# A fused two-layer residual kernel: rows of the gated blocks 8 KB apart in DRAM instead of 2 KB

## The chip, the cores and the metric

The kernel runs on one core of a Trainium2 chip. Its engines are TensorE (PE in the profile, with its weight loads as PEld), VectorE (DVE), ScalarE (ACT), GpSimd (POOL) and SyncE (SP, which here only issues transfers). Transfers between DRAM and the on-chip memories run on 16 DMA engines that all queues share. The metric is the time of one execution on the device in microseconds (us). The kernel before took 1368.03 us, the median of three runs (1366.42 to 1370.3).

## What is computed

The input x has 8 sequences of 1024 positions with 512 channels, all in 32-bit floats. Two layers are added to it in turn. Cut to what matters:

```python
# layer 0: an adapter chosen by the sequence's language, then a layer norm
h  = relu(x @ W1[lang] + b1[lang]);  a = x + h @ W2[lang] + b2[lang]
x1 = x + layernorm(a) * gamma0[lang] + beta0[lang]
# layer 1: a gate over the input and its running average, then 8 decaying sums over time
ctx   = causal_ema(x1, tau_ctx)                          # h = alpha * h + x1[t]
g     = x1 * sigmoid(concat([x1, ctx]) @ Wg.T + bg)      # the "gated" values
mod   = 0.5 + sigmoid(gelu(x1 @ Wn1.T + bn1) @ Wn2.T + bn2)   # 8 per position
trace = [causal_ema(g * mod[d], tau[d]) for d in range(8)]
temp  = sum(trace[d] * softmax(blend)[d])                # 8 traces, weights per channel
out   = (gelu(x1 @ Wsoma.T + bsoma) * sigmoid(temp @ Wtemp.T + btemp)) @ Wout.T
x     = x1 + layernorm(out) * gamma + beta
```

## The kernel before, in words

The 8192 positions are cut into 16 tiles of 512 (TOK), and a tile into four blocks of 128 positions (NB = 4, P = 128). The work is software-pipelined: slot k finishes the output of tile k-1, does the gates and traces of tile k, and prepares the input of tile k+1. Each engine has its own program, written out by hand, in a fixed order; semaphores join them. No scheduler is involved.

The part that the change touches is the way of the gated values g from one layout to another. VectorE computes g for a block with the 128 positions on the 128 partitions (`gated`, L872). For the decaying sums it needs the block in spans of 32 positions, each span repeated on four groups of 32 partitions: partition q*32 + s holds, one after the other, the rows s, 32+s, 64+s and 96+s of the block. This change of layout goes through DRAM:

- ScalarE's queue stores the block from `g` to `g_dram[b]`, 128 rows of 2 KB (`store_spans`, L529). The store of block b raises `g_stored[b]`.
- SyncE's queue waits for that (L346) and issues four loads, one for each group of 32 partitions (`repeat_spans`, L355). Each reads the whole block: 128 pieces of 2 KB, four for each partition. Blocks 0 and 2 go to `grep_0`, block 1 to `grep_1`, block 3 to the tile's x1 buffer, which is free by then.
- VectorE multiplies the repeated block by the weights of the eight traces, in four pieces (`products`, L863), each of which TensorE then takes in eight small matmuls (`within_spans`, L1158). The first piece of a block waits for the block's loads (L854).

VectorE's order in a slot is: gate work of blocks 0 and 1, then the products of block 0 with the gate work of blocks 2 and 3 between them (`gated(2)` stands after the second product of block 0), then the products of blocks 1, 2 and 3. SyncE's order is the loads of blocks 0, 1, 2, 3, then the store of the next tile's x1 to `x1_tiles` (L308), then weights and inputs of the next tile (L287 to L303). The loads of block 2 wait also for the last product of block 0 (L348), since they overwrite its buffer.

Other DRAM tensors matter as measures. `x1_tiles` has rows of 8 KB that lie 8 KB apart; it is written at L308 and read at L369. The inputs `in_x` and `in_xc` have rows of 2 KB that lie 2 KB apart; a load (L300, L303) gives each partition four of them, 256 KB apart. The rows `gamma0`, `beta0` and `b2` of the language are loaded by reading one and the same 2 KB for each of the 128 partitions (L290, L294).

Of the kernel before, what the change touches and what calls it, by code (L numbers as in the profile page):

```python
# [4 lines left out]
P = 128  # L5
BATCHES, SEQ, C = 8, 1024, 512
# [5 lines left out]
NB = TOK // P  # L12
# [28 lines left out]
def cond_resid_kernel(nc, x, xc, ids, w1, w2, b1, b2, g0, be0, wg, wn1, wsoma, wtemp, wout, wn2,  # L41
                      bg, g1, be1, cols, taus, bn2, blend, eye, bits, out):
    F = mybir.dt.float32
# [8 lines left out]
    with ctx:  # L52
# [80 lines left out]
        mv0, mv1 = (stats[:, at:at + 2 * NB].rearrange("p (b s) -> p b s", s=2) for at in (12 * NB, 14 * NB))  # L133
        rows4 = sb("rows4", [P, 4, NB])
        rstd0, rstd1, minus_half, ema_last = (rows4[:, n, :] for n in range(4))
        g_dram = nc.dram_tensor("g_blocks", [NB, P, C], F, kind="Internal").ap()
        x1_dram = nc.dram_tensor("x1_tiles", [2, P, NB * C], F, kind="Internal").ap()


# [1173 lines left out]
```

## Time and profile before

| what | value |
|---|---|
| median of three runs | 1368.03 us |
| lowest and highest run | 1366.42 and 1370.3 us |
| the profiled execution's own time | 1361.66 us |
| its span in the trace | 1359.8 us |
| TensorE busy | 1312.5 us (97%) |
| VectorE busy | 1028.8 us (76%) |
| ScalarE busy | 521.1 us (38%) |
| GpSimd busy | 373.9 us (28%) |
| mean granted TensorE clock | 0.996 of full |

The span is the time from the first to the last recorded instruction; 1.9 us of the profiled execution lie around it. A busy share is an average over all stages, so an engine at 76% can still be the one that is waited for in a part of each tile. DMA share is the mean busy share of the 16 DMA engines, and stands a little over 1 in some stretches.

### The profile page before, as it was taken

The numbers are of one execution on the slowest core, as the hardware profiler recorded it, in microseconds if no ns is written. First come the engines' busy times: TensorE is split into PE (matmuls) and PEld (weight loads), VectorE is DVE, ScalarE is ACT, GpSimd is POOL, SyncE is SP. The second block draws the span as 40 slices with busy tenths as digits, with TensorE's granted clock in tenths as the row PEclk, the third lists the DMA queues.
The fourth block names the chain that finished last, engine by engine and source line by source line (L and its number), as shares of the span: only waits on it lengthen the run. The fifth ranks groups of instructions, "written<-read, shape, count | busy, mean of one in ns | idle before, by whom it ended". The sixth has DMA issues, their size and how long they took to land.

```text
span 1359.8 us, 19735 instructions
## 1 busy us (share of the span) xinstructions
PE 1312.5 (97%) x7908; PEld 991.4 (73%) x7908; DVE 1028.8 (76%) x1526; ACT 521.1 (38%) x822; POOL 373.9 (28%) x294
## 2 busy tenths in 40 slices
PE   4889999999999999999999999999999999999997
PEld 2657778677786867768677686777868777786766
DVE  7988677887778777677786768777787786778575
ACT  3425243443524424243343433425244252434422
POOL 4405142051411404133131422304123041421102
PEclk9999999999999999999999999999999999999999
DMA  8382542907247180561706526074451825426060
GB/s 268 130 223 88 156 154 78 240 32 207 103 116 202 70 240 31 149 200 62 218 32 175 174 78 202 32 224 124 117 169 65 232 78 156 154 79 169 36 182 32
DMA packets 91486, 186.25 MB, mean 137 GB/s; under 512 B 9858, under 2 KB 14594, under 8 KB 87298
## 3 DMA queue, kind: packets, MB, share of 16 engines
q1 hardware_dynamic: 82178, 168.20, 42.4%
q10 hardware_dynamic: 9216, 16.78, 3.7%
q8 instruction: 63, 1.03, 0.3%
q14 instruction: 29, 0.24, 0.1%
HBM read 134.61 MB, written 50.33 MB: 136 GB/s over the span
## 4 chain that ended last, share of the span: by engine, by line
PE 36%; DVE 23%; DMA 16%; issue 13%; ACT 6%; SPq 2%; POOL 2%; DVEq 0%; POOLq 0%
PE ring L984 26%; DVE U L863 11%; DMA grep<-g_blocks 8%; DMA g_blocks<-g_f 7%; PE ring L977 4%; SPq L355 2%; DVE x L793 2%; DVE stats L798 2%; ACT U L523 2%; DVE g_f L872 2%; PE Tp L1158 1%; PE Tp L1169 1%; DMA x<-g_blocks 1%; POOL rows L441 1%; PE ring L1183 1%
## 5 line engine op out<-in xcount | busy, mean ns | idle before, releaser
L863 DVE TENSOR_TENSOR U<-grep,w_qs 128x1024 f32<-128x1024 f32 x192 | 227.3, 1219 | 56.9 <-issue 36.7
L412 POOL TENSOR_TENSOR x<-grep,b_row 128x512 f32<-128x512 f32 x64 | 80.5, 1289 | 547.5 <-DMA grep<-in_x 547.5
L1158 PE MATMUL Tp<-U,Arep 128*32 128x256 f32 x2048 | 133.6, 385 | 13.9 <-DVE U L863 13.2
L533 ACT ACTIVATE g_f<-g_f 128x512 f32<-128x512 f32 x64 | 40.4, 632 | 259.3 <-DVE g_f L868 259.1
L425 POOL TENSOR_TENSOR grep<-grep,beta_row 128x512 f32<-128x512 f32 x64 | 82.8, 1327 | 116.7 <-DMA grep<-x_tiles 116.6
L1158 PEld LDWEIGHTS Tp<-U,Arep 128*32 128x32 f32 x2048 | 54.1, 109 | 79.3 <-DVE U L863 39.6
L868 DVE TENSOR_TENSOR g_f<-ring,bg_row 128x512 f32<-128x512 f32 x64 | 44.1, 689 | 85.2 <-PE ring L984 85.2
L984 PE MATMUL ring<-seq_hi,Wtemp_hi 128*128 128x512 f32 x256 | 106.7, 417 | 0.1
L984 PE MATMUL ring<-x1T_hi,Wsoma_hi 128*128 128x512 f32 x256 | 103.2, 403 | 0.0
L984 PE MATMUL ring<-Wg_hi,x1T_hi 128*128 128x512 f32 x256 | 103.2, 403 | 0.0
L984 PE MATMUL ring<-Wout_hi,g_r 128*128 128x512 f32 x256 | 99.8, 390 | 1.1 <-DVE soma_r L720 1.0
L984 PE MATMUL ring<-x1T_hi,Wsoma_r 128*128 128x512 f32 x256 | 100.1, 391 | 0.0
L984 PE MATMUL ring<-Wg_hi,x1T_lo 128*128 128x512 f32 x256 | 100.1, 391 | 0.0
L984 PE MATMUL ring<-seq_hi,Wtemp_r 128*128 128x512 f32 x256 | 99.9, 390 | 0.0
L984 PE MATMUL ring<-x1T_lo,Wsoma_hi 128*128 128x512 f32 x256 | 99.9, 390 | 0.0
L984 PE MATMUL ring<-Wg_r,x1T_hi 128*128 128x512 f32 x256 | 99.8, 390 | 0.0
L984 PE MATMUL ring<-seq_lo,Wtemp_hi 128*128 128x512 f32 x256 | 99.8, 390 | 0.0
L984 PE MATMUL ring<-Wout_hi,soma_r 128*128 128x512 f32 x256 | 99.6, 389 | 0.0
L984 PE MATMUL ring<-Wout_r,g_r 128*128 128x512 f32 x256 | 99.6, 389 | 0.0
L984 PE MATMUL ring<-Wg_hi,seq_hi 128*128 128x512 f32 x256 | 99.6, 389 | 0.0
L984 PE MATMUL ring<-Wg_r,seq_hi 128*128 128x512 f32 x256 | 99.6, 389 | 0.0
L984 PE MATMUL ring<-Wg_hi,seq_lo 128*128 128x512 f32 x256 | 99.6, 389 | 0.0
(173 smaller groups left out, 2878.8 us busy)
## 6 DMA issues: line engine op xcount, KB each, us to landing
grep<-g_blocks SPq DMA_DIRECT2D x192, 256.0 KB, 4.5
grep<-in_xc SPq DMA_DIRECT2D x16, 1024.0 KB, 10.8
grep<-in_x SPq DMA_DIRECT2D x16, 1024.0 KB, 9.0
x_tiles<-x SPq DMA_DIRECT2D x16, 1024.0 KB, 9.0
g_blocks<-g_f ACTq DMA_DIRECT2D x64, 256.0 KB, 3.8
x<-g_blocks SPq DMA_DIRECT2D x64, 256.0 KB, 5.3
grep<-x_tiles SPq DMA_DIRECT2D x16, 1024.0 KB, 4.8
out<-U SPq DMA_DIRECT2D x64, 256.0 KB, 2.0
```

Of the source, the lines that this page charges most:

```text
L355: sp.dma_start(spans_of(k, b)[q * L:(q + 1) * L, :, :], g_dram[b].rearrange("(i s) c -> s i c", i=NI)).then_inc(spans_in(k, b)[0], 16)
L412: nc.gpsimd.tensor_tensor(new[:, b, :], x_t[:, b, :], b2_row[:, :], ALU.add).then_inc(xb2_ready, 1)
L425: nc.gpsimd.tensor_tensor(x1_back[:, b, :], x1_back[:, b, :], beta1_row[:, :], ALU.add).then_inc(x1b_ready, 1)
L523: nc.scalar.activation(res[:, b, :], res[:, b, :], ACT.Identity, scale=rstd1[:, b:b + 1]).then_inc(scaled_ready, 1)
L533: nc.scalar.activation(g[:, b, :], g[:, b, :], ACT.Sigmoid).then_inc(sig_ready, 1)
L793: V_.tensor_tensor(new[:, b, :], bank_of("y", k + 1, b)[:, :], new[:, b, :], ALU.add).then_inc(y_ready, 1)
L798: V_.bn_stats(stats0[:, b, :], new[:, b, :]).then_inc(ln0_step, 1)
L863: V_.tensor_tensor(U[:, (n + 2) % 4, :, :], spans_of(k, b)[:, :, at], w_qs[:, hh, at].unsqueeze(1).to_broadcast([P, NI, HC]), ALU.mult).th ...
L868: V_.tensor_tensor(g[:, b, :], bank_of("wg", k, b)[:, :], bg_row[:, :], ALU.add).then_inc(pre_ready, 1)
L977: last = nc.tensor.matmul(dst, lhsT(n), rhs(n), start=(n == 0), stop=(n == steps - 1))
L984: last = nc.tensor.matmul(dst, lhsT(a, n), rhs(b, n), start=(first and n == begin and m == 0), stop=(final and n == steps - 1 and m == 2))
L1158: last = nc.tensor.matmul(Tp[b % 2][i * L:(i + 1) * L, at], Arep[:, b * NI + i, hh, :], U[:, (n + 2) % 4, i, :], start=(hh == 0 and c == 0 ...
```

## The change

The internal DRAM tensor `g_blocks` is made four times as wide, and only the first 512 elements of each row of 2048 are used. A row of a block still has 2 KB of data, but the next row begins 8 KB further on instead of 2 KB. Within a load, the four pieces of one partition lie 256 KB apart instead of 64 KB, and a block takes up 1 MB of addresses instead of 256 KB. The number, size and order of the transfers, all other instructions and all waits are as before.

```diff
-        g_dram = nc.dram_tensor("g_blocks", [NB, P, C], F, kind="Internal").ap()
+        g_dram = nc.dram_tensor("g_blocks", [NB, P, 4 * C], F, kind="Internal").ap()[:, :, 0:C]
```

## Rows read from the trace of the kernel before

**Rows 1.** Page, parts 1, 3, 6: busy; queues; issues, KB each, us to landing.
```profile
PE 1312.5 (97%) x7908; PEld 991.4 (73%) x7908; DVE 1028.8 (76%) x1526; ACT 521.1 (38%) x822; POOL 373.9 (28%) x294
...
q1 hardware_dynamic: 82178, 168.20, 42.4%
q10 hardware_dynamic: 9216, 16.78, 3.7%
...
grep<-g_blocks SPq DMA_DIRECT2D x192, 256.0 KB, 4.5
...
g_blocks<-g_f ACTq DMA_DIRECT2D x64, 256.0 KB, 3.8
x<-g_blocks SPq DMA_DIRECT2D x64, 256.0 KB, 5.3
```

**Rows 2.** Chain that ended last, one tile: start us, length us, what.
```profile
719.85 1.43 DVE g_f L872
721.30 2.06 DMA g_blocks<-g_f
...
724.70 3.14 DMA grep<-g_blocks
727.83 3.13 issue
730.97 1.23 DVE U L863
...
733.92 0.61 DVE g_f L872
734.56 4.07 DMA g_blocks<-g_f
...
739.97 7.54 DMA grep<-g_blocks
747.53 3.15 DVE U L863 x3
```

**Rows 3.** Waits: who waited for whom, total us, times, longest us.
```profile
PEld Tp L1158 <- DVE U L863: 39.6, 59, 2.0
...
DVE U L863 <- DMA grep<-g_blocks: 15.2, 12, 3.0
...
DVE U L863 <- DMA x<-g_blocks: 2.2, 3, 1.4
```

**Rows 4.** Windows of 1 us: engines' busy us, PE clock, DMA share, GB/s; block 0's stage.
```profile
722.00:723.00 1.00, 1.00 (x6) 0.84 (x5) 0.00 (x0) 0.00 (x0) 0.00 (x0) 1.00 0.94 359
...
726.00:727.00 1.00, 1.00 (x6) 0.83 (x5) 1.00 (x2) 0.00 (x0) 0.00 (x0) 1.00 1.07 205
727.00:728.00 1.00, 1.00 (x6) 0.81 (x6) 0.82 (x1) 0.00 (x0) 0.00 (x0) 1.00 1.05 236
728.00:729.00 1.00, 1.00 (x6) 0.84 (x5) 0.00 (x0) 0.00 (x0) 0.00 (x0) 1.00 1.06 207
```

**Rows 5.** The same view while a tile of `x_tiles` is loaded (issued at 688.27).
```profile
690.00:691.00 1.00, 1.00 (x6) 0.84 (x5) 0.69 (x1) 0.16 (x1) 0.00 (x0) 1.00 0.93 385
691.00:692.00 1.00, 1.00 (x6) 0.80 (x6) 0.29 (x1) 0.66 (x1) 0.00 (x0) 1.00 1.01 426
```

**Rows 6.** Timeline of SP's queue: start us, length us, line, transfer.
```profile
744.45 1.29 SPq L308 DMA_DIRECT2D x_tiles<-x  x1
...
748.27 0.33 SPq L290 DMA_DIRECT2D b_row<-in_b  x1
748.70 0.38 SPq L294 DMA_DIRECT2D gamma_row<-in_g  x1
749.17 1.58 SPq L294 DMA_DIRECT2D beta_row<-in_be  x1
750.80 0.43 SPq L303 DMA_DIRECT2D grep<-in_xc  x1
752.19 0.39 SPq L300 DMA_DIRECT2D grep<-in_x  x1
```

**Rows 7.** Windows of 1 us after those issues, columns as in rows 4.
```profile
750.00:751.00 1.00, 0.59 (x8) 0.11 (x8) 1.00 (x2) 0.00 (x0) 0.00 (x0) 1.00 0.97 403
...
755.00:756.00 1.00, 1.00 (x17) 0.66 (x19) 1.00 (x2) 0.39 (x1) 0.00 (x0) 1.00 0.96 129
...
757.00:758.00 1.00, 0.65 (x11) 0.23 (x9) 0.90 (x2) 0.00 (x0) 0.00 (x0) 1.00 0.95 117
...
760.00:761.00 1.00, 1.00 (x6) 0.80 (x5) 0.32 (x1) 0.92 (x2) 0.00 (x0) 1.00 1.03 373
...
762.00:763.00 1.00, 1.00 (x12) 1.00 (x11) 0.45 (x2) 1.00 (x4) 0.00 (x0) 1.00 1.05 410
```

## The prediction

> **What bounds the kernel now.** I read the page's shares first. TensorE is busy for 1312.5 of 1359.8 us (97%) [rows 1], so most of the time is its matmuls, and the change doesn't touch them. What can still move the end is the 47 us in which TensorE has nothing to do, and any delay that makes those longer. So the second view is the chain of waits. In a tile from the middle of the run it goes twice through the way of the gated block over DRAM [rows 2]. For block 0: store 2.06 us, loads 3.14 us and 3.13 us of "issue", in which VectorE waits; I take these 3.13 us too for the loads, since the windows show the DMA engines full there, with a share of 1.05 and 1.06, carrying nothing but block traffic [rows 4]. Then comes `gated(2)`, and for block 2: store 4.07 us and loads 7.54 us. The reader is to see that these two ways follow one another: block 2's store can't start before VectorE has begun with block 0. The third view, the waits, tells how tightly TensorE hangs on this: it waited for VectorE's products for 39.6 us in 59 places, and VectorE for the loads of blocks 1 to 3 for 15.2 and 2.2 us, in 15 places [rows 3]. There is no slack here to swallow a slower transfer: I count each added us on a block's way, store or load, as one us of the tile, for two of the four blocks (0 and 2), hence 2 x 16 = 32 times in the run.
>
> **What the change does, part by part.**
>
> Instructions: none are added, removed or moved on any engine, and no wait changes. The packets stay the same: 9216 on ScalarE's queue for 64 stores are 144 each, that is 128 of 2 KB and 16 that signal [rows 1]. Both before and after, a row of 2 KB is the longest piece that is in one stretch on both sides, so they are neither split nor joined. Issue time and the number of packets: 0 us.
>
> The store: 256 KB is 0.262 MB. When it runs by itself its window shows 359 GB/s at a share of 0.94, which is 382 GB/s when busy, so the data takes 0.262 MB / 382 GB/s = 0.69 us of the 2.06 us [rows 2, 4]. The rest is fixed cost that a row pitch has no part in.
>
> The loads: four of 0.262 MB are 1.049 MB. In the windows of block 0 they go at 205, 236 and 207 GB/s, mean 216, with all DMA engines full [rows 4]: 4.86 us a block. That is about half of what other transfers reach (below), so something else than a plain 2 KB packet holds them. All of a load's destination lies in 32 partitions, where those other transfers have 128. I take the destination for the limit; then the DRAM side has a factor of nearly two to spare.
>
> What a pitch of 8 KB costs is not in the trace for rows of 2 KB, so it is bounded by the rows nearest to it. First, the load of a tile of x1 reads rows that begin 8 KB apart, at 385 and 426 GB/s [rows 5]; its store, which writes them, is the likeliest owner of the window with 403 [rows 6, 7]. The 16 DMA engines there all start on multiples of 8 KB, as they will for the changed blocks; but each then reads on through 8 KB, so the addresses between are used too. Second, `in_x` and `in_xc` are read in pieces of 2 KB, a partition's four pieces 256 KB apart, which is the new distance within a block load. They go at 373 to 410 GB/s [rows 6, 7]. So start addresses on multiples of 8 KB are not slow, nor is a jump of 256 KB between pieces of 2 KB. By both the transfers cost what they did: 0 us.
>
> The bound above is the loads of language rows, in which all 128 packets read the same 2 KB: the hottest spot that one can make. They go at 129 to 117 GB/s [rows 6, 7], say 123. If the new pitch were as bad, the store would take 2.13 us (+1.44) and the loads 8.53 us (+3.67), 5.11 us on a block's way and 32 x 5.11 = 164 us in all. The bound below is that the loads were held by DRAM after all, by their old distance of 64 KB, and become as fast as `in_x`, at about 390 GB/s: 2.69 us, 2.17 us less. What TensorE could get back of it is what VectorE waits for blocks 1 to 3, 17.4 us [rows 3]; block 0's gain reaches TensorE only through block 2. I take 0: the two rows near it in address pattern are at full speed, and the slow row is far from it, with one row in place of 128.
>
> The Trainium skill, in "DMA: Bandwidth & Descriptors", section "Latency and other measured facts", has a rule that speaks against this change: copies whose rows per partition lie a large power of two apart get slower, 207 GB/s at 512 KiB against about 214 at full rate, 164 at 2 MiB and 103 at 4 MiB, and padding the pitch by a few KiB cures it. No row here has so large a pitch. The new distances, 8 KB and 256 KB, are under its smallest; an estimate that gave the loads the 3% of 512 KiB would come to 0.03 x 4.86 x 32 = 5 us, and to nothing if the destination is the limit. The 256 KB of `in_x` at full rate agrees with the table's low end.
>
> Sum: 0 + 0 + 0 on the profiled execution's 1361.66 us (span 1359.8 and 1.9 around it). That execution was 6.4 us under the median of the runs; the forecast keeps to the median, so 1368 us.
>
> **What is the same.** A measurement of this kernel tells about 0.3% from no change, 4.1 us. On 32 passages that is 0.13 us each, a fifth of the store's 0.69 us: a mild slowing of the stores would already show.
>
> **Rivals.**
>
> A, slower: rows of 2 KB on multiples of 8 KB reach only part of the DRAM's paths. Now every step of 2 KB moves on to other paths; afterwards a quarter of the positions within 8 KB carries all the traffic. The price depends on how much the DRAM has to spare over the 426 GB/s seen. If the ceiling falls to half of that, 213 GB/s, the loads at 216 hardly feel it, and each store takes 1.23 us instead of 0.69: +0.54 x 32 = 17 us, 1385 us. If it falls to a quarter, 107 GB/s, the store takes 2.45 us (+1.76) and the loads 9.80 us (+4.94): 6.70 x 32 = 214 us, 1582 us; were only block 2's way to count, 107 us and 1475 us. It decides from the point where the loads fall below 216 GB/s, for they are seven times as long as the store. For it speaks that one hot row is indeed slow (117 to 129 GB/s), so a row of 2 KB is not spread over everything. Against it speak the transfers that start in step on multiples of 8 KB at full speed. They are no proof, since they go on to other addresses afterwards. Chance of the mild form 0.10, of the heavy one 0.06.
>
> B, faster: the block loads are held at 216 GB/s not by their destination but by DRAM, because pieces 64 KB apart or engines only 4 KB apart get in each other's way. The spread over 1 MB frees them. By the bound above VectorE's waits for blocks 1 to 3 go, at most 17.4 us, 1351 us; with half of it 1359 us. For it speaks that the loads are at half speed with packets of the same size as `in_x`; against it that each load fills only a quarter of the partitions, which explains the same half. Chance 0.07.
>
> C, hidden: something in the transfers changes by up to 0.13 us a block and is lost in the scatter. It is in the forecast.
>
> **How the numbers follow.** Forecast, no change, 0.77; A 0.16; B 0.07. The forecast's own range is the scatter of the runs, 1364 to 1372 us. The range that is to hold the time 8 times in 10 goes from 1361, which takes in a half of B's gain nearly, to 1385, A's mild form. The heavy form of A is left out. Faster by over 0.3%: 0.07; within it: 0.77; slower: 0.16.
>
> **What the changed profile would show.** Right: median landing of 4.5 us for the loads into grep, 5.3 for those into x and 3.8 for the stores [rows 1], all within some 0.2 us; windows of block loads again between 205 and 260 GB/s; VectorE's waits for the loads again at about 15 us; 9216 and 82178 packets. A would show first in the share of ScalarE's queue (3.7%) [rows 1], whose packets are nearly all block stores: at half speed it would be near 7%. B would show as windows of 300 GB/s and more while blocks are loaded, and shorter waits of VectorE. Wrong would be the step "0 us for the pitch" if the landing times move by more than 0.3 us, and the step "each us counts 32 times" if they move and the time doesn't.

## The result and the profile after

The kernel with rows 8 KB apart takes 1430.65 us in the median, against 1367.22 us for the kernel before: a ratio of 1.0439, 95% interval 1.0387 to 1.0492. That is 63 us slower by these medians of four runs each. One of the changed kernel's four ran at a granted clock of 0.752 and took 1652.53 us; the ratio leaves it out, and by the ratio the loss is 60 us. The forecast was no change, 1368 us, with a range up to 1385 us.

The profiled execution took 1432.35 us, its span is 1430.6 us, 70.8 us more than before. The page's parts 1, 3 and 6 of the changed kernel, in the columns of [rows 1]:

```profile
PE 1337.9 (94%) x7908; PEld 995.7 (70%) x7908; DVE 1030.8 (72%) x1526; ACT 521.7 (36%) x822; POOL 373.0 (26%) x294
...
q1 hardware_dynamic: 82178, 168.20, 41.4%
q10 hardware_dynamic: 9216, 16.78, 3.1%
...
grep<-g_blocks SPq DMA_DIRECT2D x192, 256.0 KB, 5.3
...
g_blocks<-g_f ACTq DMA_DIRECT2D x64, 256.0 KB, 4.2
x<-g_blocks SPq DMA_DIRECT2D x64, 256.0 KB, 8.2
```

The packets are the same in number. The stores land 0.4 us later than in [rows 1], the loads of blocks 0 to 2 0.8 us and those of block 3 2.9 us. The share of ScalarE's queue did not rise, it fell from 3.7 to 3.1%: this share counts the time that packets occupy a DMA engine. The packets of block 0's store begin 0.93 us after its issue and take 0.79 us in both kernels (medians over the 16 tiles, from the times of the trace's single packets); but from the end of the last packet to the landing it is 0.35 us before and 0.73 us after. So the store's loss is a wait behind its packets, and the share doesn't hold it. The sign that the prediction named for its rival A, a share near 7%, did not come though the rival did.

The chain that ended last, in one tile, as in [rows 2] (start us, length us, what):

```profile
758.94 2.45 DMA g_blocks<-g_f
...
762.73 2.74 DMA grep<-g_blocks
765.47 4.23 issue
769.70 1.23 DVE U L863
...
773.30 5.01 DMA g_blocks<-g_f
...
779.65 7.06 DMA grep<-g_blocks
786.73 3.15 DVE U L863 x3
```

From the issue of block 0's store to its first product it is 10.76 us; before it was 730.97 - 721.30 = 9.67 us. Over the 16 tiles the median of this time went from 8.85 to 10.6 us. I call it the block's way below, since every experiment can be measured by it. The windows of 1 us in that stage, columns as in [rows 4]:

```profile
764.00:765.00 1.00, 1.00 (x6) 0.84 (x5) 1.00 (x2) 0.00 (x0) 0.00 (x0) 1.00 0.85 186
765.00:766.00 1.00, 1.00 (x6) 0.84 (x5) 0.46 (x1) 0.00 (x0) 0.00 (x0) 1.00 0.82 199
766.00:767.00 1.00, 1.00 (x6) 0.81 (x5) 0.00 (x0) 0.00 (x0) 0.00 (x0) 1.00 1.14 188
767.00:768.00 1.00, 1.00 (x6) 0.84 (x5) 0.00 (x0) 0.00 (x0) 0.00 (x0) 1.00 0.60 186
```

They carry 186 to 199 GB/s, where [rows 4] have 205 to 236. These are the even middle of the stage; from the start of block 0's first load packet to the end of its last it is 4.86 us before and 6.31 us after (medians over the tiles), which for 1.049 MB is a mean of 216 and 166 GB/s. The share is the thing to look at: 0.60 to 0.85 in three of the four, where it was 1.05 to 1.07. On the mean the DMA engines are no longer full, so I take something behind them to hold the loads. The view has the mean of the 16 engines only: whether all of them wait a little or some stand idle, it doesn't show.

The waits (who waited for whom, total us, times, longest us), as in [rows 3]:

```profile
PEld Tp L1158 <- DVE U L863: 85.5, 92, 2.1
...
DVE U L863 <- issue: 62.4, 16, 5.4
...
DVE U L863 <- DMA grep<-g_blocks: 55.7, 28, 4.6
```

The second row is the wait for block 0, which before was 36.7 us in part 5 of the profile's page; the third was 15.2 us in [rows 3], all of it for block 2, of whose wait there are now 47.6 us. Their sum grew by 25.7 + 40.5 = 66.2 us. So VectorE waits 66.2 us longer for block loads, in a span that is 70.8 us longer. The first row passes this on to TensorE: its wait for the products was 39.6 us in [rows 3]. TensorE's time with nothing to do grew from 47.3 to 92.7 us, by 45.4 us; the other 25.4 us of the 70.8 are in its busy time.

Part of that busy time is the clock. The mean granted clock of TensorE is 0.984 in this execution where it was 0.996. Windows around one place where it fell:

```profile
443.00:444.00 1.00, 0.00 (x0) 0.00 (x0) 1.00 (x2) 0.49 (x1) 0.00 (x0) 1.00 1.00 211
...
447.00:448.00 1.00, 0.94 (x14) 0.20 (x8) 1.00 (x3) 0.00 (x0) 0.00 (x0) 0.50 1.08 394
...
440.00:450.00 10.00, 7.15 (x48) 3.60 (x48) 7.20 (x7) 2.17 (x4) 0.00 (x0) 0.81 1.04 304
450.00:457.00 7.00, 7.00 (x54) 4.92 (x52) 3.27 (x4) 1.79 (x3) 0.00 (x0) 0.79 0.69 255
457.00:464.00 7.00, 7.00 (x43) 6.00 (x42) 5.54 (x7) 5.88 (x10) 2.75 (x3) 1.00 0.31 119
```

In the window from 440 to 450 us TensorE was busy for 7.15 of 10 us, as it waited for block 2's products, and at 443 us it did nothing at all. Then the clock fell to 1.2 instead of 2.4 GHz (0.50 in the window at 447 us); in the window from 457 us it is full again. Over the whole execution the clock lost 0.016 x 1430.6 - 0.004 x 1359.8 = 17 us of full-speed time, which is the most that it can have cost; it overlaps with the waits and can't be added to them. Not all of it is due to the change: only two of the stretches at the low clock, at 446 and 965 us, lie in the middle of the run, 6.8 us long each, and the others are in the first 100 and the last 40 us, where e1 below, with hardly any loss, has as many within its first 100 us. The profile of the kernel before shows the upper end of what that kernel gets: timed beside the experiments it has mean clocks of 0.989 to 0.996, the changed kernel 0.984 to 0.990 in three executions.

### The profile page after: what moved, and what is told of

It is laid out like the page before. It is cut to its first block, busy times and chain, and to the rows that moved or that the text cites. A ratio compares the mean times of both kernels' runs of the same rounds, so it can differ in the third digit from the quotient of the medians.

```text
span 1430.6 us, 19735 instructions
## 1 busy us (share of the span) xinstructions
PE 1337.9 (94%) x7908; PEld 995.7 (70%) x7908; DVE 1030.8 (72%) x1526; ACT 521.7 (36%) x822; POOL 373.0 (26%) x294
## 3 DMA queue, kind: packets, MB, share of 16 engines
q1 hardware_dynamic: 82178, 168.20, 41.4%
q10 hardware_dynamic: 9216, 16.78, 3.1%
## 4 chain that ended last, share of the span: by engine, by line
DVE 25%; PE 24%; DMA 19%; issue 16%; ACT 7%; SPq 3%; POOL 2%; DVEq 0%; POOLq 0%
PE ring L984 15%; DVE U L863 12%; DMA grep<-g_blocks 9%; DMA g_blocks<-g_f 8%; PE ring L977 3%; SPq L355 3%; DVE x L793 3%; DMA x<-g_blocks 3%; ACT U L523 3%; DVE stats L798 2%; DVE g_f L872 2%; POOL rows L441 1%; PE Tp L1169 1%; ACT L533 1%; PE ring L1183 1%
## 5 line engine op out<-in xcount | busy, mean ns | idle before, releaser
L1158 PE MATMUL Tp<-U,Arep 128*32 128x256 f32 x2048 | 143.8, 391 | 48.0 <-DVE U L863 47.2
L1158 PEld LDWEIGHTS Tp<-U,Arep 128*32 128x32 f32 x2048 | 51.1, 109 | 126.1 <-DVE U L863 85.5
## 6 DMA issues: line engine op xcount, KB each, us to landing
grep<-in_xc SPq DMA_DIRECT2D x16, 1024.0 KB, 11.7
```

What stands on the lines that cost most here:

```text
L1158: last = nc.tensor.matmul(Tp[b % 2][i * L:(i + 1) * L, at], Arep[:, b * NI + i, hh, :], U[:, (n + 2) % 4, i, :], start=(hh == 0 and c == 0 ...
```

## The experiments

Each was timed against the kernel before on the same chip; a "so many us over" below is the difference of the two medians taken there. Block 0's way is the median over 16 tiles from the issue of its store to its first product in the profiled execution, and block 2's way the same for block 2.

| run | distance of rows | ratio, 95% interval | block 0's way, us | block 2's way, us |
|---|---|---|---|---|
| before | 2 KB | 1 | 8.85 | 11.3 |
| changed | 8 KB | 1.0439, 1.0387 to 1.0492 | 10.6 | 13.3 |
| e1 | 10 KB | 1.0046, 1.0022 to 1.0070 | 8.8 | 11.8 |
| e2 | 8 KB, blocks side by side | 1.0464, 1.0421 to 1.0506 | 10.3 | 13.8 |
| e3 | 4 KB | 1.0142, 1.0097 to 1.0187 | 9.5 | 12.2 |
| e4 | 32 KB | 1.0080, 1.0050 to 1.0110 | 9.0 | 11.7 |
| e5 | control, loads of x, 2 KB | 0.9997, 0.9975 to 1.0020 | 8.85 | 11.2 |
| e6 | 8 KB in the store only | 1.0091, 1.0058 to 1.0124 | 9.3 | 11.8 |
| e7 | 8 KB in the load only | 1.0627, 1.0598 to 1.0656 | 10.6 | 14.7 |
| e8 | 8.5 KB | 1.0067, 1.0046 to 1.0089 | 9.0 | 11.8 |
| e9 | load: 2 KB, pieces 256 KB apart | 1.0003, 0.9978 to 1.0027 | 9.0 | 11.6 |
| e10 | load: 8 KB, pieces 254 KB apart | 1.0054, 1.0029 to 1.0079 | 9.1 | 11.7 |
| e11 | 16 KB | 1.0143, 1.0106 to 1.0181 | 9.4 | 12.3 |
| e12 | 2 KB, groups 0, 2, 1, 3 | 0.9938, 0.9913 to 0.9962 | 8.4 | 11.0 |
| e13 | 8 KB, groups 0, 2, 1, 3 | 1.0395, 1.0352 to 1.0438 | 10.4 | 13.0 |

**e1: rows 10 KB apart.**

```diff
-        g_dram = nc.dram_tensor("g_blocks", [NB, P, C], F, kind="Internal").ap()
+        g_dram = nc.dram_tensor("g_blocks", [NB, P, 5 * C], F, kind="Internal").ap()[:, :, 0:C]
```

> Rows of the blocks 10 KB apart: the addresses are spread wider still (1.25 MB a block), but successive rows fall on different positions modulo 8 KB. Theory P (position): rows on multiples of 8 KB all fall on one part of the DRAM's paths, which gives the block loads about 188 GB/s where they had 216. Then 10 KB frees them: about 1368 us, block loads back at 205 to 236 GB/s, landing 4.5 us. Theory S (spread): every row of 2 KB that lies apart from its neighbours costs something, whatever the distance is a multiple of. Then the time stays at 1425 us or more and the loads at about 188 GB/s.

Measured 1368.87 us, 4.6 us over the kernel before. The rows are spread more widely than in the changed kernel and nearly all of the loss is gone. Windows in block 0's stage:

```profile
822.00:823.00 1.00, 1.00 (x6) 0.84 (x5) 1.00 (x2) 0.00 (x0) 0.00 (x0) 1.00 1.03 234
823.00:824.00 1.00, 1.00 (x6) 0.81 (x6) 0.39 (x1) 0.00 (x0) 0.00 (x0) 1.00 1.09 221
824.00:825.00 1.00, 1.00 (x6) 0.84 (x5) 0.00 (x0) 0.00 (x0) 0.00 (x0) 1.00 1.00 219
```

Rate and share are again those of [rows 4]. Theory S, that spreading by itself costs, falls as the main cause; it may own the remaining 0.5%.

**e2: the four blocks side by side.**

```diff
-        g_dram = nc.dram_tensor("g_blocks", [NB, P, C], F, kind="Internal").ap()
+        g_dram = nc.dram_tensor("g_blocks", [P, NB, C], F, kind="Internal").ap().rearrange("p b c -> b p c")
```

> The four blocks of a tile lie side by side: row p holds the 2 KB of block 0, then those of blocks 1, 2 and 3. So a block's rows are 8 KB apart as in the changed kernel, but the tensor has 1 MB in all as before, and nothing is left unused. Theory P: a block's own transfers still hit one quarter of the positions, and a block's loads run mostly by themselves, so it is about as slow as the changed kernel, 1415 to 1431 us; where transfers of two blocks overlap they use different quarters, which may give a little back. Theory S: the rows of one block lie just as far apart, but every 8 KB is used by the four blocks in turn; if it is the size of the area that costs, 1368 us, if it is the distance within a transfer, 1431 us.

1426.36 us, 62.1 us over. The tensor is as small as before and has no unused gaps, and the whole loss is there. It is the distance within one transfer that counts, not the size of the area. The tensor in this run looks perfectly dense; nothing in its shape warns.

**e3: rows 4 KB apart** (`2 * C` in the line of e1).

> Rows 4 KB apart. Theory P: two of the four positions modulo 8 KB are used, so the ceiling is about twice the 188 GB/s seen at 8 KB, well above the 216 GB/s at which the loads go for another reason. About 1368 us, within 0.5%. Theory S: a cost that grows with the distance gives a part of the 63 us, some 1385 to 1410 us.

1383.79 us, 19.5 us over. Theory P had it at no loss, S at 17 to 42 us over the 1368. S has this number, though e1 speaks against it as the main cause; P is wrong here: it gave the loads too much room, since it thought of one ceiling that either binds or doesn't.

**e4: rows 32 KB apart** (`16 * C`).

> Rows 32 KB apart, 4 MB a block. Theory P with a period of 8 KB: the same quarter as at 8 KB, so the same time, 1420 to 1435 us. Theory P with a longer period, of which 8 KB left a quarter or less in use: a further loss, block loads near or under 100 GB/s and a time above 1550 us. Theory S: slower than at 8 KB by some tens of us.

1374.15 us, 9.9 us over. None of the three expectations has this. Theory P with a fixed period of 8 KB falls: at 32 KB every row also begins on a multiple of 8 KB. So, if P's picture of places is right at all, higher bits of the address have a part in where a row falls. Theory S wanted more than at 8 KB, and falls too.

**e5, e6, e7: which side carries it.** In these the loads read rows of the input x instead of the stored blocks (the decaying sums are then of x), so that the two sides can be changed apart. e5 is the control; e6 has the wide tensor of the changed kernel for the stores; e7 reads every fourth row of x.

```diff
 # e5 and e6, and in e6 also the line of the change itself
-                                     g_dram[b].rearrange("(i s) c -> s i c", i=NI))
+                                     x[k].rearrange("(b p) c -> b p c", b=NB)[b].rearrange("(i s) c -> s i c", i=NI))
 # e7
+                                     x[k].rearrange("(p b) c -> b p c", b=NB)[b].rearrange("(i s) c -> s i c", i=NI))
```

> Control for the next two. Stores of the blocks as in the kernel before (rows 2 KB apart); the loads read the same number of 2 KB rows, 2 KB apart, from the input x instead of the stored blocks, so the decaying sums are computed of x and not of the gated values. All waits are kept. Both theories: 1365 us within 0.5%, as the kernel before, if it makes no difference that the rows read are not just written ones.

> Stores with rows 8 KB apart, loads from the input x with rows 2 KB apart (decaying sums are of x, as in the control). Theory L (loads carry the loss): only the stores' part, median landing 2.06 to 2.45 us for block 0 in one tile, 0.39 us x 32 = 12 us over the control, about 1377 us. Theory W (writes carry it, and slow the reads that follow): most of the 63 us, above 1405 us.

> Stores with rows 2 KB apart, loads from the input x with rows 8 KB apart, a partition's four rows 256 KB apart (decaying sums are of x in another order). Theory L: some 45 to 55 us over the control, 1410 to 1420 us, block loads again near 175 to 190 GB/s with the DMA engines not full. Theory W: under 15 us over the control.

The control gives 1365.25 us, no difference. The stores alone give 1377.51 us, 11.4 us over; 12 were expected. The loads alone give 1451.92 us, 85.8 us over: theory L holds in kind, but it had 45 to 55 us, and the loss is larger than that of both sides together in the changed kernel. In block 0's way the two runs don't differ (10.6 us); the difference lies in the later blocks, of which block 2's way is 14.7 us against 13.3. The block windows of e7:

```profile
781.00:782.00 1.00, 1.00 (x6) 0.84 (x5) 1.00 (x2) 0.00 (x0) 0.00 (x0) 1.00 0.89 168
782.00:783.00 1.00, 1.00 (x6) 0.83 (x5) 0.67 (x1) 0.00 (x0) 0.00 (x0) 1.00 0.97 201
783.00:784.00 1.00, 1.00 (x6) 0.82 (x5) 0.00 (x0) 0.00 (x0) 0.00 (x0) 1.00 0.80 150
784.00:785.00 1.00, 1.00 (x6) 0.84 (x5) 0.00 (x0) 0.00 (x0) 0.00 (x0) 1.00 0.95 209
```

Their mean is 182 GB/s, under the 190 of the changed kernel's windows, and block 0's load packets take 6.70 us from first to last, against 6.31. Why x is read somewhat slower still at this distance isn't settled; another part of the DRAM, and rows not just written, are both possible.

**e8: rows 8.5 KB apart** (`4 * C + P`).

> Rows 8.5 KB apart (8 KB and 512 bytes), 1.06 MB a block. Theory P (the position of a row within 8 KB decides, and the positions come round in steps of some hundred bytes): successive rows shift by 512 bytes, so 16 rows cover all positions, and the time is back to about 1368 us. If the part that a row falls on is decided in steps of 2 KB or more, four successive rows share a part and the engines, which start some rows apart, are spread only partly: 1375 to 1400 us. If only the distance counts: 1425 us or more.

1376.81 us, 10.7 us over. 512 bytes more take away five sixths of the loss. It lies in the range of the second expectation, a partial spread (1375 to 1400 us), at its low edge.

**e9 and e10: the two distances of a load.** The change moved the rows of neighbouring partitions from 2 to 8 KB apart and the four pieces of one partition from 64 to 256 KB. Both runs load from x and are to be held against e5.

```diff
 # e9: neighbours 2 KB apart, pieces 256 KB
+                                     x[k].rearrange("(i b s) c -> b s i c", i=NI, b=NB)[b])
 # e10: neighbours 8 KB apart, pieces 254 KB
+                                     x[k][b:b + 508].rearrange("(i r) c -> r i c", i=NI)[0:125:4])
```

> Loads from the input x as in the control; a partition's four rows lie 256 KB apart, but rows of neighbouring partitions 2 KB apart (decaying sums are of x, other computation kept). Separates the two distances that the change moved together. Theory R (the 8 KB between partitions costs): as the control, 1365 us within 0.5%, block windows about 272 GB/s. Theory J (the jump of 256 KB between the pieces of a partition costs): 1430 to 1452 us, as with rows 8 KB apart.

> Loads from the input x; rows of neighbouring partitions 8 KB apart, a partition's four rows 254 KB apart, so that each falls on another of the four places within 8 KB (decaying sums are of x). Theory B (balance over the transfer decides): the four places get a quarter of each load each, about 1365 to 1375 us. Theory T (what the engines hit at one moment decides): the 16 engines begin on the same place and go on in step, so much of the loss stays, 1400 us or more.

e9 is at 1366.32 us, a ratio of 1.0003: the jump of 256 KB costs nothing. e10 is at 1371.84 us, 7.5 us over. It differs from e7 by 2 KB in the jump between a partition's pieces, and that takes away 78 of 86 us. Windows of e10:

```profile
818.00:819.00 1.00, 1.00 (x6) 0.81 (x5) 0.57 (x1) 0.40 (x1) 0.00 (x0) 1.00 1.08 248
819.00:820.00 1.00, 1.00 (x6) 0.82 (x5) 1.00 (x2) 0.00 (x0) 0.00 (x0) 1.00 1.02 219
820.00:821.00 1.00, 1.00 (x6) 0.84 (x5) 0.26 (x1) 0.00 (x0) 0.00 (x0) 1.00 1.15 238
```

Neighbouring partitions are 8 KB apart, and yet the rate is full and the DMA engines are full. Of the two theories only B has this time: what a transfer hits over its whole length decides. That is an inference; T supposed that the engines go on in step, and no view here shows whether they do.

**e11: rows 16 KB apart** (`8 * C`).

> Stores and loads of the blocks with rows 16 KB apart, 2 MB a block. It lies between 8 KB (+63 us) and 32 KB (+10 us). If every doubling mixes in a further address bit that spreads the rows: about the middle, 1385 to 1410 us. If 8 KB is the one bad distance: 1370 to 1380 us. If 16 KB is worse, as a fixed period of 8 KB or more with half the places again would make it: above 1440 us.

1387.22 us, 22.9 us over. It is the first of the three expectations (1385 to 1410 us). With e3 and e4 this makes 8 KB a peak: 1.4, 4.4, 1.4 and 0.8% at 4, 8, 16 and 32 KB. The loss falls on both sides, and every value is clear of noise.

**e12: what holds the loads at 216 GB/s.**

```diff
-                    for q in range(NQ):
+                    for q in (0, 2, 1, 3):
```

> The kernel before, with the four loads of a block issued in the order of partition groups 0, 2, 1, 3 instead of 0, 1, 2, 3. Tests the prediction's step that the destination in 32 partitions holds the block loads at 216 GB/s. If groups 0 and 1 share one part of the way into the memory and groups 2 and 3 another, neighbouring loads now use both: block loads faster than 216 GB/s, up to about 390, and 1350 to 1362 us. If DRAM or the packets hold them, or the groups share the way otherwise: 1365 us within 0.4% and the same rate.

1355.88 us, ratio 0.9938 (0.9913 to 0.9962): faster than the kernel before, and the fastest of all. Part 6 of its page in the profile, and its waits:

```profile
grep<-g_blocks SPq DMA_DIRECT2D x192, 256.0 KB, 4.1
...
x<-g_blocks SPq DMA_DIRECT2D x64, 256.0 KB, 4.4
```
```profile
DVE U L863 <- issue: 29.9, 15, 2.7
...
DVE U L863 <- DMA grep<-g_blocks: 1.6, 3, 1.1
```

The loads land 0.4 and 0.9 us sooner than in [rows 1], and VectorE's waits for the loads into grep fell from 15.2 us [rows 3] to 1.6. Nothing moved in DRAM; only the order of the destinations did. So the destination, or the order in which it is filled, did have a part in the limit. Block 0's windows stay at 221 to 266 GB/s, far from 390, so it isn't the only one.

**e13: the same order with rows 8 KB apart** (the changed kernel with the edit of e12).

> The changed kernel (rows 8 KB apart) with the loads of a block issued in the order of partition groups 0, 2, 1, 3. With rows 2 KB apart this order took about 0.6% off, so there the destination held the loads. Theory D (two limits, the lower one holds: destination 216 GB/s, DRAM at 8 KB about 188 GB/s): the other order frees only the destination, so it brings nothing here, 1425 to 1435 us. Theory M (with rows 8 KB apart the destination still slows the loads, both add up): it brings as much as before or more, 1405 to 1420 us.

1415.20 us, ratio 1.0395. The order brings 0.4% here (1.0439 to 1.0395) and 0.6% at 2 KB; the intervals overlap, so that it brings anything at 8 KB isn't certain. If it does, it speaks for theory M, that both limits act. The waits are those of the changed kernel, less a little:

```profile
DVE U L863 <- issue: 60.2, 16, 5.1
DVE U L863 <- DMA grep<-g_blocks: 51.9, 28, 4.0
```

## Why the prediction was wrong

**The path, 32 passages.** This step held. In the changed kernel block 0's way is 10.6 - 8.85 = 1.75 us longer and block 2's 13.3 - 11.3 = 2.0 us; 16 times both is 60 us, the loss by the ratio. In e7 the same sum is 82 us against 85.8, in e6 15 against 11.4, in e12 -12 against -8.4, and in no run is it more than 6 us from the difference of the medians, though the ways come from one execution each. That there is no slack to swallow a slower transfer was right.

**Packets and issue, 0 us.** Right: 82178 and 9216 packets as before.

**The destination as the limit of the loads.** Right in part (e12). But the conclusion "then the DRAM side has a factor of nearly two to spare" did not follow. It was true for rows 2 KB apart and says nothing of rows at another distance. At 8 KB the loads go at about 190 GB/s in the middle windows and at 166 on the mean, under the 216 at which rival A was said to decide.

**The price of the 8 KB, 0 us.** This is the step that failed: block 0's loads took 6.31 us instead of 4.86 by their packets, and its store landed 2.45 instead of 2.07 us after its issue. The sign that the prediction set for it, landing times that move by more than 0.3 us, came. I bounded it by the two rows nearest in pattern and took their value: x1's tiles, whose rows begin 8 KB apart [rows 5], and the inputs with jumps of 256 KB [rows 6, 7]. Both readings of the trace were right, and e9 confirms that the jump is free. But neither transfer leaves out any place: the first reads all 8 KB of each row, the second has rows 2 KB apart. I had noted this ("no proof, since they go on to other addresses afterwards") and still let it carry the forecast. The argument from engines that start in step on multiples of 8 KB was about the moment, and e10 speaks for the balance over the whole transfer. In the changed kernel all 128 rows of a block begin on multiples of 8 KB and end 2 KB later, and 6 KB out of every 8 are never touched; no transfer in the trace before was like that. By itself this doesn't explain the size, since at 16 and 32 KB still more is left out and less is lost.

Within the same step, the store was split into 0.69 us of data and a rest "that a row pitch has no part in". It was the other way round: the packets take as long as before, and the 0.38 us are all in the rest, between the last packet and the landing.

**The upper bound.** The one hot row at 123 GB/s [rows 7] was the better measure after all: it shows that few places give a low ceiling, and the result, a mean of 166 GB/s, lies between it and the 216.

**Rival A.** Its mechanism, a part of the DRAM's paths carrying all of the traffic, fits what was seen, as far as it goes, with corrections. Its two forms, 213 and 107 GB/s, left out the one that came between them. At the mean of 166 GB/s that the loads had (6.31 us, +1.45), its own working gives the store 0.262 / 0.166 = 1.58 us of data (+0.89), in all 75 us against 60: the store's term was too large, since 0.38 us were measured and none of it in the data. And it spoke of a fixed quarter of the positions within 8 KB, which e4 and e11 refute. Its sign, a share of ScalarE's queue near 7%, failed because the store's loss isn't in the packets.

**Rival B.** Its mechanism, DRAM at 64 KB as the limit, is shown by no run, and two speak against it: with pieces 256 KB apart (e9) and with neighbours 10 KB apart (e1) the loads are no faster. Half of its price came for another cause: it gave faster loads up to 17.4 us, and e12 got 8.4.

**The rule of the Trainium skill** ("DMA: Bandwidth & Descriptors", section "Latency and other measured facts") on large power-of-two distances was set aside because its table begins at 512 KiB. This case shows a loss at 8 KB that is larger than at 32 KB, so the table can't be read as growing from a harmless small end. Its figures are for copies of 16 KiB per partition between DRAM tensors, which no run here has. The cure that the Trainium skill names, padding by a few KiB, worked: 10 KB in place of 8 (e1).

Open is why 8 KB is the worst distance. That higher address bits are mixed in is inferred from e4 and e11; which bits wasn't measured. Open too is why the loads of e7 are slower still, and whether all 16 DMA engines wait alike.

## What to carry to other kernels

A transfer of short rows at a wide distance has to be judged by the set of places that it touches, not by the distances found in other transfers that touch everything in between; where the trace has no such set, the price is unknown, and the range should say so. If DMA engines are not full (share 0.6 to 0.85) in a stage that moves nothing but one kind of transfer, look behind them, at the memory: here a changed distance (10 KB in place of 8, or even 8.5) took nearly all of the loss away, as did a jump of 254 KB in place of 256 between the pieces. And the order in which loads fill groups of partitions is worth a try: it gave 0.6% here for one line. Where a path repeats, measure it in each of its places: block 0's way alone would have left the loss of e7 unexplained.

## What the runs showed of the hardware that was not expected

- 2 KB rows that lie 8 KB apart are read at 186 to 199 GB/s in the windows shown, where the same number of rows 2 or 10 KB apart goes at 205 to 236 GB/s. The time of the kernel rises by 4.4%, with 4 or 16 KB by 1.4%, with 32 KB by 0.8%.
- The slowing isn't seen in the busy share of the queue that writes: 3.7% before, 3.1% after, while the stores land 0.4 us later. The last packet of block 0's store ends at the same time after its issue, and the landing follows 0.73 us later instead of 0.35.
- Loads issued to partition groups 0, 2, 1, 3 land in 4.1 us instead of 4.5.
